# Splitting the pooled product of a two-layer conditional kernel into three f32r passes on one core

## The reference, cut to what matters

```python
attn_in = tanh(x @ W1 + b1)                  # W1: 512 x 128
scores = attn_in @ v                         # one score per token
p = softmax(where(mask, scores, -1e30))      # 128 x 128 per block
x = x + (p @ x) / mask.sum(-1)               # first layer
x = x + x @ W[cat] + b[cat]                  # second layer
```

## Time and profile before

| | |
|---|---|
| median of 3 runs | 347.25 us (347.15 to 347.75) |
| the profiled execution's own time | 348.24 us |
| its span | 346.5 us |
| busy: TensorE / its weight loads | 328.6 us (95%) / 239.4 us (69%) |
| busy: VectorE / ScalarE | 245.0 us (71%) / 257.0 us (74%) |
| mean granted TensorE clock | 0.98 |

### The profile page before, as it was taken

One profiled execution on the slowest core, in us unless ns is written; L12 is line 12 of the kernel. 1 busy time (PEld: TensorE's weight loads), 2 busy tenths in 40 slices (PEclk: granted clock), 3 DMA queues, 4 the chain that ended last, 5 costly groups with the idle time before them and its releaser, 6 DMA issues.

```text
span 346.5 us, 4558 instructions
## 1 busy us (share of the span) xinstructions
PE 328.6 (95%) x1352; PEld 239.4 (69%) x1352; DVE 245.0 (71%) x225; ACT 257.0 (74%) x373; POOL 4.7 (1%) x19
## 2 busy tenths in 40 slices
PE   7473999999999999999999999999999999999996
PEld 5252777777767777777776777777777777777773
DVE  1559679594949769494968859494977949495810
ACT  2568387795968777795978779696977779596832
POOL 5000000000000000000000000000000000000000
PEclk9969699999999999999999999999999999999999
DMA  6999768999899888989898898989889899863113
GB/s 162 354 424 421 283 257 285 348 307 377 271 303 338 298 341 289 373 291 341 293 308 331 289 347 301 383 291 332 309 274 363 283 357 308 310 210 129 62 61 121
DMA packets 21641, 101.55 MB, mean 293 GB/s; under 512 B 2706, under 2 KB 2706, under 8 KB 11634
## 3 DMA queue, kind: packets, MB, share of 16 engines
q1 hardware_dynamic: 21458, 100.94, 80.3%
q0 software_dynamic: 160, 0.33, 0.9%
HBM read 84.48 MB, written 16.78 MB: 292 GB/s over the span
## 4 chain that ended last, share of the span: by engine, by line
PE 89%; DMA 4%; DVE 3%; SPq 2%; issue 1%; ACT 0%; DVEq 0%
PE ps_y L489 17%; PE ps_y L490 16%; PE ps_y L491 16%; PE ps_y L500 16%; PE ps_pre L456 13%; PE ps_y L502 4%; DMA w_raw<-in_L_cond_W 4%; PE ps_scores L464 4%; PE ps_pT L477 2%; DVE w_lo L359 1%; PE ps_scores L466 1%; DVE xT_lo L346 1%; DVE w_raw L335 1%; SPq L176 0%; SPq L153 0%
## 5 line engine op out<-in xcount | busy, mean ns | idle before, releaser
L359 DVE TENSOR_TENSOR w_lo<-w_raw,w_hi 128x2048 fp32r<-128x2048 f32 x63 | 143.9, 2284 | 0.1
L251 ACT ACTIVATE w_hi<-w_raw 128x2048 fp32r<-128x2048 f32 x63 | 121.8, 1934 | 4.3 <-DVE w_raw L335 4.3
L489 PE MATMUL ps_y<-w_hi,xT_hi 128*128 128x512 f32 x256 | 104.1, 407 | 5.2 <-DVE w_lo L352 4.9
L490 PE MATMUL ps_y<-w_lo,xT_hi 128*128 128x512 f32 x256 | 101.2, 395 | 0.0
L491 PE MATMUL ps_y<-w_hi,xT_lo 128*128 128x512 f32 x256 | 100.4, 392 | 0.0
L500 PE MATMUL ps_y<-z_sb,mix 128*128 128x512 f32 x128 | 65.2, 591 | 0.0
L489 PEld LDWEIGHTS ps_y<-w_hi,xT_hi 128*128 128x128 f32 x256 | 48.8, 191 | 19.3 <-DVE w_lo L352 5.3
L364 DVE TENSOR_REDUCE neg_max<-ps_scores 128x4 f32<-128x512 f32 x16 | 11.1, 692 | 69.7 <-PE ps_scores L466 69.7
L491 PEld LDWEIGHTS ps_y<-w_hi,xT_lo 128*128 128x128 f32 x256 | 48.5, 190 | 11.1
L490 PEld LDWEIGHTS ps_y<-w_lo,xT_hi 128*128 128x128 f32 x256 | 48.6, 190 | 9.2
L502 PE MATMUL ps_y<-b_both,one_hot 128*128 128x512 f32 x64 | 50.8, 794 | 0.0
(11 more groups left out here) (58 smaller groups left out, 174.2 us busy)
## 6 DMA issues: line engine op xcount, KB each, us to landing
w_raw<-in_L_cond_W SPq DMA_DIRECT2D x63, 1024.0 KB, 7.4
out<-out_sb SPq DMA_DIRECT2D x64, 256.0 KB, 5.0
x_raw<-in_x SPq DMA_DIRECT2D x15, 1024.0 KB, 9.2
x_raw<-in_x SPq DMA_DIRECT2D x2, 512.0 KB, 6.1
w_raw<-in_L_cond_W SPq DMA_DIRECT2D x2, 512.0 KB, 9.8
w_raw<-in_L_cond_W SPq DMA_DIRECT2D x1, 256.0 KB, 7.1
b_raw<-in_L_cond_b POOLq DMA_DIRECT2D x2, 128.0 KB, 8.3
type_all<-in_itok_B POOLq DMA_DIRECT2D x1, 32.0 KB, 6.8
```

The lines of the kernel that those rows point to most:

```text
L251: nc.scalar.activation(w_hi[k % NH][:], w_raw[k % NW][:], ACT.Copy).then_inc(w_hi_ready, 1)
L359: nc.vector.tensor_tensor(w_lo[k % NL][:], w_raw[k % NW][:], w_hi[k % NH][:].bitcast(F32), ALU.subtract).then_inc(w_lo_ready, 1)
L489: nc.tensor.matmul(y[:], xT_hi[q][:, c, xs], w_hi[k % NH][:, c, :], start=(c == 0), stop=False)
L490: nc.tensor.matmul(y[:], xT_hi[q][:, c, xs], w_lo[k % NL][:, c, :], start=False, stop=False)
```

## The change

`z_sb` becomes `z_hi` and `z_lo`, and `mix` becomes `mix_hi` and `mix_lo`, all f32r. ScalarE's two copies now write the upper halves. VectorE gets the lower halves as new work: one subtraction per block (`split_z_lo`) and one per group (`split_mix_lo`), each reading a PSUM bank and the upper half, 128x512 elements. In VectorE's loop they stand behind `split_w_lo` and ahead of `add_identity`. The single f32 product of `pz` becomes three f32r matmuls. On ScalarE the copy of the transposed softmax moves ahead of `copy_out`. On VectorE `max_group` is written ahead of `split_xT_lo`.

```diff
-        z_sb = [sb(f"z_sb{i}", [P, D], F32) for i in range(NZ)]
+        z_hi = [sb(f"z_hi{i}", [P, D], F32R) for i in range(NZ)]
+        z_lo = [sb(f"z_lo{i}", [P, D], F32R) for i in range(NZ)]
...
-        mix = [sb(f"mix{i}", [P, G, S], F32) for i in range(2)]
+        mix_hi = [sb(f"mix_hi{i}", [P, G, S], F32R) for i in range(2)]
+        mix_lo = [sb(f"mix_lo{i}", [P, G, S], F32R) for i in range(2)]
...
                 if 1 <= k <= B:
-                    copy_z(k - 1)
+                    split_z_hi(k - 1)
+                if k < B and (b == 1 and g >= 1 or k == 2):
+                    split_mix_hi(g)
                 if k >= 3:
                     copy_out(k - 3)
                 if b == 0 and g + 1 < GROUPS:
                     split_xT_hi(g + 1)
-                if k < B and (b == 1 and g >= 1 or k == 2):
-                    copy_mix(g)
...
+            def split_mix_lo(g):
+                dve.wait_ge(mix_hi_ready, g + 1)
+                nc.vector.tensor_tensor(mix_lo[g % 2][:], ps_pT[:].rearrange("p (b j) -> p b j", b=G),
+                                        mix_hi[g % 2][:].bitcast(F32), ALU.subtract).then_inc(mix_lo_ready, 1)
+
+            def split_z_lo(k):
+                dve.wait_ge(z_hi_ready, k + 1)
+                nc.vector.tensor_tensor(z_lo[k % NZ][:], ps_y[k % NY][:], z_hi[k % NZ][:].bitcast(F32),
+                                        ALU.subtract).then_inc(z_lo_ready, 1)
...
-            for k in range(B):
+            for k in range(B + 1):
                 g, b = k // G, k % G
                 if k == 0:
                     max_group(0)
+                if b == 3 and g + 1 < GROUPS:
+                    max_group(g + 1)
                 if b == 1 and g + 1 < GROUPS:
                     split_xT_lo(g + 1)
-                if b == 3 and g + 1 < GROUPS:
-                    max_group(g + 1)
                 if k + 2 < B:
                     split_w_lo(k + 2)
+                if k < B and (b == 1 and g >= 1 or k == 2):
+                    split_mix_lo(g)
+                if k >= 1:
+                    split_z_lo(k - 1)
                 if k + 4 < B:
                     add_identity(k + 4)
...
                 if g >= 1:
-                    pe.wait_ge(mix_ready, g)
+                    pe.wait_ge(mix_lo_ready, g)
...
-                pe.wait_ge(z_ready, k + 1)
-                pe.wait_ge(mix_ready, g + 1)
-                nc.tensor.matmul(y[:], mix[g % 2][:, b, :], z_sb[k % NZ][:], start=False, stop=False,
-                                 skip_group_check=True)
+                pe.wait_ge(z_lo_ready, k + 1)
+                pe.wait_ge(mix_lo_ready, g + 1)
+                mh, ml = mix_hi[g % 2][:, b, :], mix_lo[g % 2][:, b, :]
+                nc.tensor.matmul(y[:], mh, z_hi[k % NZ][:], start=False, stop=False, skip_group_check=True)
+                nc.tensor.matmul(y[:], ml, z_hi[k % NZ][:], start=False, stop=False, skip_group_check=True)
+                nc.tensor.matmul(y[:], mh, z_lo[k % NZ][:], start=False, stop=False, skip_group_check=True)
```

More of the change, by code:

```diff
@@ L133, in program @@
         probsT_done = sem("probsT_done")
-        mix_ready = sem("mix_ready")
+        mix_hi_ready = sem("mix_hi_ready")
+        mix_lo_ready = sem("mix_lo_ready")
         xw_done = sem("xw_done")
-        z_ready = sem("z_ready")
+        z_hi_ready = sem("z_hi_ready")
+        z_lo_ready = sem("z_lo_ready")
         pz_done = sem("pz_done")
@@ L266, in exp_group, with split_mix_hi @@
                 last.then_inc(exp_ready, 1)
-            def copy_mix(g):
+            def split_mix_hi(g):
                 act.wait_ge(probsT_done, g + 1)
@@ L271, in copy_mix, with split_z_hi @@
                     act.wait_ge(pz_done, G * (g - 1))
-                nc.scalar.activation(mix[g % 2][:], ps_pT[:].rearrange("p (b j) -> p b j", b=G), ACT.Copy)\
-                    .then_inc(mix_ready, 1)
-            def copy_z(k):
+                nc.scalar.activation(mix_hi[g % 2][:], ps_pT[:].rearrange("p (b j) -> p b j", b=G), ACT.Copy)\
+                    .then_inc(mix_hi_ready, 1)
+            def split_z_hi(k):
                 act.wait_ge(xw_done, k + 1)
@@ L278, in copy_z @@
                     act.wait_ge(pz_done, k - NZ + 1)
-                nc.scalar.activation(z_sb[k % NZ][:], ps_y[k % NY][:], ACT.Copy).then_inc(z_ready, 1)
+                nc.scalar.activation(z_hi[k % NZ][:], ps_y[k % NY][:], ACT.Copy).then_inc(z_hi_ready, 1)
             def copy_out(k):
```

## The result

The changed kernel takes 335.83 us (median of 4 runs, 335.46 to 336.75) against 347.5 us for the kernel before on the same chip. The ratio is 0.9667, with a 95% interval of 0.9642 to 0.9691: 3.3% faster. The forecast was 336.35 us. The profiled execution took 336.02 us with a span of 334.2 us, 12.3 us less than before.

The account below looks back on a forecast made before the run. The prediction took TensorE to bound the kernel: 64 blocks saving 0.17 us each give 10.9 us, all else free, so the median 347.25 us becomes 336.35 us. The range was 333.4 to 340.0 us.

Parts of the forecast that it names:

- What bounds the kernel: Over a group of 19.75 us every piece of the chain is TensorE's; VectorE has 4.63 us spare before max_group.
- The price of a pass: At pz, three f32r matmuls of 0.23 us replace 0.86 us, saving 0.17 us per block, 10.9 us over 64.
- The start: Before pz(0), the new subtractions are done at 40.7 and wanted at 42.79: free by 2 us.
- The price of a new VectorE operation: Each 128x512 subtraction with a PSUM source costs 0.61 us start to start; five add 3.05 us per group.
- VectorE's cover by its sum: VectorE works 18.17 us of a 19.07 us group, keeping 0.90 us of idle time.
- The order within a group: Walk of VectorE's queue: no step late; smallest slack on TensorE's path 0.7 us, xT_lo ahead of hidden.
- my condition for trouble: VectorE becomes the bound at 0.79 us per new operation; all of the gain is gone at 0.93 us.
- The order swap, ScalarE, the transfers: Swapping max_group and split_xT_lo, earlier mix_hi with later copy_out on ScalarE, and later loads and stores all cost nothing.
- The rival on transfers: Loads and stores at 320 GB/s hold a group at 19.7 us, 347 us in total; chance 0.03.
- The end: After the last xw, z_lo(63) is done in about 1.4 us against 1.84 us before pz(63): free by 0.4 us.
- VectorE as the bound: At 0.86 us per new operation VectorE sets a group of 19.42 us, 342.3 us in total; chance 0.09.
- A PSUM read held up by other engines: New VectorE operations cost above 0.93 us; at 1.2 us the kernel takes 367.8 us; chance 0.04.

Follow-up runs that it names:

- two subtractions outside the loop: Changed kernel with z_lo of blocks b = 0 and 1 done twice, between split_xT_lo and the next max_group: 338.5 us, ratio 0.9728.
- the two runs without idle time: Changed kernel with every z_lo subtraction done twice, 355.5 us, and with only those of blocks b = 0 and 1 done twice, 338.5 us.
- two-pass kernel: Changed kernel without the second matmul of the product (mix_lo with z_hi left out): 326.18 us, ratio 0.9373.
- the run with `xT_lo` earlier: Changed kernel without the mix_lo with z_hi matmul, and with split_xT_lo moved ahead of add_identity of the pass before: 321.76 us, ratio 0.9241.
- the run with the extra operations inside the loop: Changed kernel with z_lo of blocks b = 2 and 3 done twice, between max_group and split_xT_lo: 348.36 us, ratio 1.0009.

## Why the prediction was right, step by step

- **What bounds the kernel.** Right. TensorE had no gap in a group before or after; VectorE's extra work alone moved nothing (ratio 1.0) and leaving it out moved nothing (0.9681 against 0.9667, intervals overlapping).
- **The price of a pass.** Mechanism right, size a little small. I took 0.23 us; three take 0.68 us, so a block saves 0.18 us by its pieces. From the first product's start to the last one's end (300.51 us before, 288.65 us after) the loss of time is 11.9 us, 0.185 us per block, where the term was 10.9 us. Of the 0.75 us that a group lost, four products give 0.72 us and `hidden` 0.02 us (2.80 to 2.78). The 216 ns for 512 columns of the Trainium skill ("TensorE: Matmul & The Clock Gate", Back-to-back issue gap), which that section gives for a matmul by itself, are not what f32r matmuls show here: in the new product they stand 0.91 / 4 = 0.2275 us apart, the dearer side that I had taken.
- **The start.** I put it at nothing; it gave about 0.35 us. `hidden` of the second group runs partly at a low granted clock. The rows of both kernels, before first:

```profile
34.61 5.42 PE ps_pre L456 x12
```

```profile
34.76 4.95 PE ps_pre L474 x12
```

  In the stretch 37 to 40 us the mean granted clock was 0.52 before and 0.67 after, where 0.5 is the level of 1.2 GHz and 1.0 that of 2.4 GHz; TensorE had waited ahead of `hidden` in both. TensorE had been busy for only 0.66 us from 30 to 34 us before, and for 1.12 us after. Other variants of the changed kernel took from 4.46 us (two matmuls swapped) to 5.33 us (two subtractions outside the loop) for the same matmuls, the kernel with the subtractions alone 5.42 us. So this scatter is not the change's, and the 0.35 us are luck. With the 0.1 us at the end the sum is 11.9 + 0.35 + 0.1 = 12.3 us, the difference of the spans.
- **The price of a new VectorE operation.** Right: 0.60 us from start to start with a PSUM source. The extra 65 ns that the Trainium skill gives for it ("VectorE: DVE Perf Modes", The TRN2 errata) do not show here: `add_identity` with two SBUF sources takes 0.60 us too (172.47 to 173.07).
- **VectorE's cover by its sum.** Forecast 0.90 us of idle time, shown 0.92. But the true spare time is 1.00 us, as the two runs without idle time say (18.00 and 18.02 us of work).
- **The order within a group.** The walk found the right place, `xT_lo` ahead of `hidden`, but not what it meant. It gave 0.7 us of slack there; in the trace `xT_lo` ends at 169.16 and `hidden` stands in the chain at 169.94, 0.78 us later. The records show less:

```profile
166.87 2.29 DVE L350 TENSOR_TENSOR xT_lo<-x_raw,xT_hi 128x2048 fp32r<-128x2048 f32 x1
169.55 0.19 PEld L474 LDWEIGHTS ps_pre<-xT_hi,w_hi 128*128 128x128 f32 x1
169.78 0.39 PE L474 MATMUL ps_pre<-xT_hi,w_hi 128*128 128x512 f32 x1
```

  I had read the start of the piece in the earlier trace rows as the start of the work; the matmul starts 0.16 us earlier, and its weight load 0.39 us behind the end of `xT_lo`. In the stalled two-pass kernel that load came 0.11 us behind it, so by this estimate 0.28 us are usable; the lengths of the loop give 0.33 us. So my condition for trouble, 0.79 us per operation by the sum, was not the first to be met: two subtractions lie in the loop, and by this estimate (0.33 / 2) + 0.60 = 0.77 us each would have begun to cost.
- **The order swap, ScalarE, the transfers.** Nothing, as forecast: with the order undone the ratio is 0.9651, and no wait for a transfer appears in the steady groups. The rival on transfers, a pace of 19.7 us, is out: with the same loads and stores a group took 18.09 us in the run with `xT_lo` earlier.
- **The end.** Free, as forecast: the last three products follow each other without a gap. The product at 340.02 in the earlier trace rows is not the last one but that of block 61; the last starts at 342.20, and the prediction's 1.84 us count from the right place.
- **The rivals.** VectorE as the bound was a real danger, 0.33 us per group away; the run with the extra operations inside the loop shows what it does, at ratio 1.0009. A PSUM read held up by other engines, the mechanism named for a loss, did not show: the new operations cost 0.60 us.

## What to carry to other kernels

When work is moved onto an engine that has spare time, add up its queue, then follow each loop of waits through the engines with its own slack: the smaller of the two is the cover, and here it was a third of the idle time shown. Idle time in front of one instruction says nothing of an instruction earlier in the queue that someone waits for. And when two engines come within a few per cent of each other, move the waited-for instruction ahead of one that is not urgent before touching the amount of work. That was worth 4.4 us in the two-pass kernel, which its loop held; in the changed kernel TensorE's own 19.00 us are longer than the loop, so nothing is to be expected there, and it was not tried.

## What the runs showed of the hardware

- A wait that ends just before 12 matmuls takes away the head start of the first weight load: in the two-pass kernel it starts 0.03 us before its matmul, in the changed kernel, at 169.55, 0.23 us ahead of one at 169.78. The second matmul then follows 0.31 us after the first, and the 12 take 2.88 us instead of 2.78 us up to the next matmul. The chain shows 3.04 us and counts the rest of the stall as matmul time, not as a wait.
- An f32 product of 512 columns takes 0.86 us, three f32r passes 0.68 us. At the full granted clock, the start of an f32r matmul stood 0.225 us (L521 to L522) to 0.234 us (L522 to the next L474) behind the one before, as means of the pairs from 64 to 280 us. What sets the difference was not found.
- An f32r matmul with the same stationary operand as the one before it had its own weight load all the same, 64 of 64 at 188 ns.
